# Two-layer LoRA product in one pass: the start of the first block product is put in another order

## The reference

```python
# layer 0: ids 0, W0 = L0 base_weight, A0, B0 picked per batch entry
x = x + (x @ W0.T + b0) + (x @ A0[ids].T) @ B0[ids].T
# layer 1: W1, A1, B1, SCALING = 2
x = x + (x @ W1.T + b1) + 2 * (x @ A1[ids]) @ B1[ids]
```

## Time and profile before

| | us |
|---|---|
| median of 3 runs | 2081.53 (2079.79 to 2082.87) |
| profiled execution, its own time | 2081.34 |
| its span, first to last instruction | 2079.6 |
| TensorE busy in the span | 2054.9 (99%) |
| first matmul of step 0 | 19.7 |

### The profile page before, as it was taken

The page is one execution under the profiler, slowest core; times in us unless marked ns, Lnnn a source line. Parts: engine busy times, 40 slices in busy tenths (PEclk is TensorE's granted clock), DMA queues, the critical chain, the costliest instruction groups (busy, mean ns, idle before and its releaser), DMA issues.

```text
span 2079.6 us, 27886 instructions
## 1 busy us (share of the span) xinstructions
PE 2054.9 (99%) x9372; PEld 1709.6 (82%) x9372; DVE 1588.2 (76%) x2180; ACT 725.5 (35%) x1291; POOL 717.3 (34%) x513
## 2 busy tenths in 40 slices
PE   6999999999999999999999999999999999999999
PEld 6887888888888888888888888888888888888887
DVE  5688868877888887677877677877687886777895
ACT  5572323323333333333333333333333333333332
POOL 2134414551304552213544131545040445131443
PEclk9999999999999999999999999999999999999999
DMA  9986748995737795746796655798564789474676
GB/s 295 283 313 176 249 139 260 285 297 158 239 109 242 241 315 175 216 126 207 235 311 215 186 170 163 225 296 273 146 214 135 215 267 321 145 220 119 218 218 195
DMA packets 283898, 458.03 MB, mean 220 GB/s; under 512 B 27500, under 2 KB 88940, under 8 KB 283244
## 3 DMA queue, kind: packets, MB, share of 16 engines
q1 hardware_dynamic: 215788, 333.54, 52.1%
q10 hardware_dynamic: 67968, 122.71, 19.3%
HBM read 382.75 MB, written 74.45 MB: 220 GB/s over the span
## 4 chain that ended last, share of the span: by engine, by line
PE 90%; DVE 3%; issue 1%; DMA 1%; SPq 0%; POOL 0%; ACT 0%; DVEq 0%; POOLq 0%; ACTq 0%
PE acc L1568 28%; PE acc L1574 28%; PE acc L1579 28%; PE h_acc L1492 2%; PE h_acc L1496 2%; PE acc L1506 1%; PE h_acc L1495 1%; DVE w_lo L1083 0%; DVE vp_lo L1078 0%; DMA w_raw<-v_t 0%; DVE c_acc L1191 0%; DMA x_pre<-w_t 0%; DVE xop_lo L1109 0%; DVE x_sum L1098 0%; DVE c_out L1261 0%
## 5 line engine op out<-in xcount | busy, mean ns | idle before, releaser
L893 POOL TENSOR_TENSOR w_raw<-w_raw,w_second 128x512 f32<-128x512 f32 x464 | 654.5, 1411 | 1222.8 <-DMA w_second<-wc_t 696.1
L1083 DVE TENSOR_TENSOR w_lo<-w_raw,w_hi 128x512 fp32r<-128x512 f32 x672 | 582.0, 868 | 420.3 <-ACT w_hi L930 417.7
L930 ACT ACTIVATE w_hi<-w_raw 128x512 fp32r<-128x512 f32 x672 | 424.3, 632 | 1234.7 <-PE acc L1579 1048.5
L1568 PE MATMUL acc<-xop_hi,w_hi 128*128 128x512 f32 x2688 | 726.1, 391 | 1.1 <-DVE c_pre L1261 1.1
L1574 PE MATMUL acc<-xop_lo,w_hi 128*128 128x512 f32 x2688 | 723.2, 390 | 0.0
L1579 PE MATMUL acc<-xop_hi,w_lo 128*128 128x512 f32 x2688 | 722.0, 390 | 0.0
L1579 PEld LDWEIGHTS acc<-xop_hi,w_lo 128*128 128x128 f32 x2688 | 503.9, 188 | 104.0
L1574 PEld LDWEIGHTS acc<-xop_lo,w_hi 128*128 128x128 f32 x2688 | 504.1, 188 | 103.3
L1568 PEld LDWEIGHTS acc<-xop_hi,w_hi 128*128 128x128 f32 x2688 | 503.3, 188 | 103.8 <-ACT w_hi L930 1.5
L1109 DVE TENSOR_TENSOR xop_lo<-x_sum,xop_hi 128x512 fp32r<-128x512 f32 x240 | 158.5, 681 | 3.8 <-ACT xop_hi L943 3.0
L1261 DVE TENSOR_TENSOR c_out<-acc,c_out 128x512 f32<-128x512 f32 x224 | 149.7, 680 | 4.4 <-PE acc L1506 3.8
(11 more groups left out here) (105 smaller groups left out, 1017.9 us busy)
## 6 DMA issues: line engine op xcount, KB each, us to landing
w_raw<-wc_t SPq DMA_DIRECT2D x448, 256.0 KB, 3.9
w_second<-wc_t ACTq DMA_DIRECT2D x320, 256.0 KB, 4.4
w_raw<-v_t SPq DMA_DIRECT2D x208, 256.0 KB, 4.2
w_second<-v_t ACTq DMA_DIRECT2D x144, 256.0 KB, 4.8
x_in<-x_t SPq DMA_DIRECT2D x128, 256.0 KB, 5.8
out_t<-c_out SPq DMA_DIRECT2D x128, 256.0 KB, 5.3
w_part<-w_t SPq DMA_DIRECT2D x32, 512.0 KB, 8.0
x_pre<-w_t SPq DMA_DIRECT2D x64, 256.0 KB, 6.0
```

What stands on the lines that cost most here:

```text
L893: nc.gpsimd.tensor_tensor(w_raw[:, r, :], w_raw[:, r, :], w_second[:, n % RAW2, :], ALU.add if sign > 0 else ALU.subtract).then_inc(w_summ ...
L930: nc.scalar.activation(flat(w_hi[:, s % RING, :, :]), w_raw[:, r, :], ACT.Copy).then_inc(w_hi_ready, 1)
L1083: nc.vector.tensor_tensor(flat(w_lo[:, s % RING, :, :]), w_raw[:, s % RAW, :], f(flat(w_hi[:, s % RING, :, :])), ALU.subtract).then_inc(w_ ...
L1568: nc.tensor.matmul(bank[:, :], w_hi[:, s % RING, kk, :], xop_hi[:, place, :], start=(k == 0), stop=False)
```

## The change

What moves (step numbers are TensorE's):

- Transposes of the identity, whose result nobody reads (`keep_clock`): 16 ahead of parts 0 and 1, 20 behind them.
- The turn of parts: none in step 1, two parts in each step from 2 to 15; pair 4 now ahead of pair 3 but behind pair 2. Groups of 4 transposes behind 6, 8, 10 and 12 matmuls (step 0: 4, 5, 8, 10).
- A1 products: those of parts 0 to 3 in steps 2 and 3 instead of 1 and 2; the later ones still two steps behind the turn. The first of a step stands behind 8 matmuls, the second behind all 12. The split of a part stands in the step of its product instead of one step before.
- b0_rows are turned in step 2 (`B_IN`): two banks in its middle, two behind it.
- X's first four tiles have DMAs and a semaphore of their own, issued right behind parts 0 and 1; parts 2 and 3 come next, then X's second half, two of the eight a1 DMAs, parts 4 and 5, the stores of parts 0 and 1, and only then b0_rows. The ids go from ScalarE's queue.
- ScalarE splits X's first tiles around w_split_hi(0), copies parts 2 and 3 before a1_hi, and splits X's tiles 4 to 7 after a1_hi and split_part_hi(0). b1_hi moves from the end of its iteration 3 to the end of iteration 4, behind e_hi; b0t's splits and the store of b0t move from 2 to 3.

```diff
+    A1_BY_ACT = 6
-    B_AFTER, E_AFTER, Q_AFTER = (0, 1), 3, (5, 6)
+    B_IN, E_AFTER, Q_AFTER = 2, 3, (5, 6)
-    TURN_AT = ((0, (-1, -1, 0, 0)), (1, (1, 1, 2, 2)), (4, (3, 3, 4, 4)), (2, (5, 5, 6, 6)), (5, (7, 7, 8, 8)),
-               (3, (9, 9, 10, 10)), (6, (11, 11, 12, 12)), (7, (13, 14, 15, 15)))
+    TURN_AT = ((0, (-1, -1, 0, 0)), (1, (2, 2, 3, 3)), (2, (4, 4, 5, 5)), (4, (6, 6, 7, 7)), (3, (8, 8, 9, 9)),
+               (5, (10, 10, 11, 11)), (6, (12, 12, 13, 13)), (7, (14, 14, 15, 15)))
-    PART_G_AT = [max(at + 2, 1) for _, _, at in PARTS]
+    PART_G_AT = [2, 2, 3, 3] + [at + 2 for _, _, at in PARTS[4:]]
-        return [n for n in range(2, NPART) if PART_G_AT[n] == g + 1]
+        return [n for n in range(2, NPART) if PART_G_AT[n] == g]
...
# SyncE, start
             for n in range(2):
                 load_part(n)
-            for k in range(KH):
-                load_x(0, 1, 1, k)
+            row = KH * P
+            for o in range(TT):
+                sp.dma_start(flat(x_pre[:, 3, o, 0:KS, :]), w1_t[TT + o, :, row:row + SW]).then_inc(x_first_loaded, 16)
             for n in range(2, PIN):
                 load_part(n)
+            for o in range(TT):
+                load_x(0, 1, 1, 2 * o + 1)
             sp.wait_ge(ids_loaded, 32)
+            for b in range(A1_BY_ACT, BATCH):
+                sp.dma_start(a1_raw[:, b, :, :], ...).then_inc(a1_sp_loaded, 16)
+            for n in PARTS_AT[-1]:
+                load_part(n + PIN)
+            for n in PARTS_AT[-1]:
+                store_part(n)
             for b in range(BATCH):
                 sp.dma_start(b0_rows[b * RANK:(b + 1) * RANK, :], ...).then_inc(b0_loaded, 16)
...
# ScalarE, start
+            for n in PARTS_AT[0]:
+                for mm in range(2):
+                    copy_part(n, mm)
+            act_e.wait_ge(a1_loaded, A1_BY_ACT * 16)
+            act_e.wait_ge(a1_sp_loaded, (BATCH - A1_BY_ACT) * 16)
             nc.scalar.activation(a1_hi[:, :, :, :], ...)
+            split_part_hi(0)
+            for k in range(KS, KH):
+                x_split_hi(0, k)
...
# TensorE
+            def keep_clock(n):
+                for _ in range(n):
+                    nc.tensor.transpose(h_acc[:, 0:P], ident[:, :], ident[:, :])
             pe.wait_ge(ident_made, 2)
+            keep_clock(16)
             for n in PARTS_AT[-1]:
                 for mm in range(2):
                     turn_part(n, mm)
+            keep_clock(20)
...
-                    for n in range(NPART):
-                        if PART_G_AT[n] == s:
-                            add_part_g(n)
-                    turn_at = {0: (), 2: (0, 6), 4: (0, 3, 6, 9) if s > 0 else (0, 1, 2, 3)}[len(turns)]
+                    turn_at = {0: (), 2: (0, 6), 4: (6, 8, 10, 12) if s > 0 else (4, 5, 8, 10)}[len(turns)]
+                    products = [n for n in range(NPART) if PART_G_AT[n] == s]
...
# behind the matmuls with xop_lo, ahead of those with w_lo
+                    for n in products[:1]:
+                        add_part_g(n)
+                    if s == B_IN:
+                        pe.wait_ge(b0_loaded, BATCH * 16)
+                        for n in range(2):
+                            turn(n, [...])
...
# behind the step
+                    for n in products[1:]:
+                        add_part_g(n)
+                    turn_before(3 * KS)
+                    if s == B_IN:
+                        for n in range(2, 4):
+                            turn(n, [...])
```

More of the change, by code:

```diff
@@ L756, in _ @@
                     load_w(s)
-                if g < 2:
-                    for b in range(4 * g, 4 * g + 4):
+                if 1 <= g < 3:
+                    for b in range(4 * (g - 1), 4 * g):
                         sp.dma_start(b1_rows[b * RANK:(b + 1) * RANK, :],
@@ L940, in x_split_hi @@
                 else:
-                    wait_x(act_e, q, 0)
+                    if q == 0 and k < KS:
+                        act_e.wait_ge(x_first_loaded, 16 * KS)
+                    else:
+                        wait_x(act_e, q, 0)
                     src = x_tile(q, 0, k)
@@ L1004, in load_second @@
                                 ).then_inc(wb_loaded[n % RAW2], 16)
+            for l, ids_d in enumerate((ids0, ids1)):
+                act_e.dma_start(ids[0:1, l, :], ids_d.rearrange("(o n) -> o n", o=1)).then_inc(ids_loaded, 16)
             act_e.wait_ge(ident_made, 2)
@@ L1009, in _ @@
             act_e.wait_ge(ids_loaded, 32)
-            for b in range(BATCH):
+            for b in range(A1_BY_ACT):
                 slot = act_e.value_load(ids[0:1, 1, b:b + 1], min_val=0, max_val=SLOTS - 1)
@@ L1031, in _ @@
                 pl, i = divmod(q, NPROD)
+                for n in PARTS_AT[g] if g == B_IN else []:
+                    for mm in range(2):
+                        copy_part(n, mm)
                 if g + 2 < NG:
@@ L1034, in _ @@
                 load_second(g + 2 + RAW2)
+                if g == 1:
+                    split_part_hi(1)
+                for n in PART_ENDS:
+                    if PART_G_AT[n] == g - 1:
+                        copy_part_g(n)
                 for n in parts_split(g)[:1]:
                     split_part_hi(n)
-                for n in PART_ENDS:
-                    if PART_G_AT[n] == g:
-                        copy_part_g(n)
                 for n in parts_split(g)[1:]:
                     split_part_hi(n)
[L1042 to L1045, removed]
+                if g == 3:
                     act_e.wait_ge(t_copied, 4)
@@ L1050, in _ @@
                                          .broadcast_to([P, KT, 2]), ACT.Copy).then_inc(b0t_hi_ready, 1)
+                for n in PARTS_AT.get(g, []) if g not in (0, B_IN) else []:
+                    for mm in range(2):
+                        copy_part(n, mm)
                 if g == 3:
@@ L1053, in _ @@
                     a_split_hi(0)
+                if g == 4:
+                    act_e.wait_ge(e_masked, 1)
+                    nc.scalar.activation(e_hi[:, :], e_bd[:, :], ACT.Copy).then_inc(e_hi_ready, 1)
                     act_e.wait_ge(b1_loaded, BATCH * 16)
@@ L1186, in scale_c @@
                 if k == 0:
-                    dve.wait_ge(x_loaded[block_no(half, th)], (pl + 1) * 16 * KH)
+                    wait_block(dve, block_no(half, th), pl)
                     if half == pl:
@@ L1274, in _ @@
                     nc.vector.tensor_copy(v_part[:, n, mm, :], part_bank[mm][:, :]).then_inc(part_copied, 1)
[L1275 to L1278, removed]
+            w_split_lo(0)
             for k in range(KS):
                 x_split_lo(0, k)
+            w_split_lo(1)
             dve.wait_ge(a1_hi_ready, 1)
@@ L1289, in _ @@
                 pl, i = divmod(q, NPROD)
+                if g in (B_IN, B_IN + 1):
+                    for n in range(2 * (g - B_IN), 2 * (g - B_IN) + 2):
+                        t_copy(n, flat(b0t_raw[:, 4 * n:4 * n + 4, :]))
                 if g + 2 < NG:
@@ L1296, in _ @@
                         evict(qq, m)
+                if g == 1:
+                    split_part_lo(1)
                 for n in parts_split(g):
                     split_part_lo(n)
[L1299 to L1302, removed]
+                if g == 3:
                     dve.wait_ge(t_copied, 4)
@@ L1575, in _ @@
                                          start=False, stop=False)
+                    for n in products[:1]:
[3 more added lines that the diff above has]
+                        for n in range(2):
+                            turn(n, [b0_rows[:, (4 * n + i) * P:(4 * n + i + 1) * P] for i in range(4)])
                     pe.wait_ge(w_lo_ready, s + 1)
```

51 lines of the change are left out of this document (22 added, 29 removed).

## The result

The changed kernel takes 2114.41 us, median of 5 runs (2112.33 to 2115.53), against 2081.77 (2079.79 to 2082.87) for the kernel before, also 5 runs: ratio 1.0153, 95% interval 1.0142 to 1.0164. It is 32.6 us slower, far outside the predicted range, which ended at 2090. The profiled span is 2112.7 us against 2079.6. A change of 0.2%, 4.2 us, is about what a single run can tell.

A forecast was written before the change was run, and what follows sets the result against it. TensorE, busy 99% of the span, was taken as the bound, so only idle time and clock could change. 2081.34 + 2.45 (make_q later) + 1.6 + 0.8 (clock) - 1.3 (steps 6 to 17) gave 2084.9 us, range 2076.5 to 2090.

The forecast's parts named there:

- Steps 6 to 17: Later steps: short waits of 2.5 us in all replace 3.8 us lost before, 1.3 us gained.
- The text's own sign of being wrong: Wrong if make_q starts at 66 or below, or if steps 6 to 17 idle for much over 3 us.
- Clock: Slow clock behind TensorE's idle stretches: 1.6 us a fall; 1.6 for step 5, 0.8 for step 2; bounds 0 and 6.4.
- Start: Step 0 starts at 13.25, not 19.7, and ends near 18.35 with a warm clock; head start 9.7 us.
- Before step 2: TensorE idles from 21.1 to 24.7 for ScalarE's list up to w_hi(2); product 0 ends at 28.7.
- B0's rows: Middle of step 2: b0 lands at 31.1 (bounds 28.0 and 33.4), so TensorE idles from 28.7.
- the rival in which the transposes do not count: Start: idle transposes do not warm the clock, step 0 runs at half clock, product 0 ends at 31.6; 2085.4 us; chance 0.10.
- Step 5: Product 6 waits for vp_lo(6) from 61.5 to 65.0, 3.5 us idle; make_q starts at 70.25.
- Idle transposes: Start: 36 at 0.22 us, 7.9 us, end at 12.9, before step 0 at 13.25; costed at nothing.
- The head start is spent: At make_q: 75.0 with 4.75 us of moved work counted, against 72.57 before, 2.45 us later.
- slow clock: Rival: each idle stretch over 1.4 us up to step 5 drops the clock, no later gain; 2090.2 us; chance 0.22.
- head start survives: Rival: b0 lands by 28.7, no clock falls in steps 2 and 5, later wait gone; -4.3, 2077.1 us; chance 0.18.

The follow-up runs named there:

- experiment 1: Kernel before, with only the late places of products, turns and splits from step 6 on: 2105.21 us, 21.6 above the kernel before.
- experiment 2: Changed kernel with products, turns and splits from step 6 on back in their old places: 2083.44 us, 0.2 from the kernel before.
- experiment 5: Changed kernel with b1_hi moved behind the splits of iteration 5: 2112.54 us, 1.9 less.
- experiment 3: Changed kernel with ScalarE's splits of X and a ahead of the second part's copies in steps 10 to 15: 2101.74 us, 12.7 less.
- experiment 4: Changed kernel with GpSimd's residual additions of the first product cut to one column in 128: 2113.61 us, no change.
- experiment 6: Changed kernel without the 36 idle transposes: 2112.65 us, 1.8 less.
- experiment 8: Changed kernel with turns from step 6 on behind 0, 3, 6 and 9 matmuls again, products and splits left late: 2102.13 us, 12.3 less.
- experiment 9: Changed kernel with splits for products of step 6 on one step ahead again, products and turns left late: 2104.74 us, 9.7 less.
- experiment 10: Kernel of experiment 2 plus b1_hi late, 46 idle transposes and part 2's split between copies of parts 4 and 5: 2079.52 us, ratio 0.9993.
- experiment 7: Changed kernel with 46 instead of 20 idle transposes behind part 1: 2114.95 us.

## Why the prediction was wrong

**The step that failed is "Steps 6 to 17"**, forecast at 1.3 us of gain with bounds of 3.8 gained and 2 lost, measured at 27.85 lost. It let "copy_part_g (0.4), vp_hi and vp_lo need 2.9 us behind the last product", with an eviction where there is one. That is not the list. What counts is everything that ScalarE and VectorE have between the step's last copy and the end of the split: at step 15 7.3 us, from 166.76 to 174.02. The rows for it were in the trace of before, where the same list takes the same 7.26 us; the wait of 2.22 us at 159.63, which the forecast counted as saved, was this chain. The change took the slack away in two ways at once: the last turn, and with it the last copy, went to the end of the step, and the split went from the step before into the product's own. The product's later place gave back only two thirds of a step. The bounds came from the same short list, so the range could not hold the result either, and none of the rivals was this chain. The text's own sign of being wrong (idle of much over 3 us in steps 6 to 17) is what came: 23.74 us. In experiment 1 these places alone cost 21.6 us, and in experiment 2 their removal gives back 31. The middle stretches give 22.9 and 30.4 us for the same two; of the difference, 3.5 us are idle time and 4.0 busy time at a lower clock. Part of it goes with the turns: the old lists turn one part in each of steps 13 and 14, the new ones two, and the waits in steps 14 and 15 are 0 and 0.74 us in experiment 1 against 1.38 and 5.01. The rest was not settled.

**Clock.** A fall was priced at 1.6 us, and two were counted. The middle stretch has 7.0 us of it, all set off by waits that the forecast did not have. In step 5 the fall did come, at 1.4 us by experiment 5. The rows are steps 5, 11, 12 (no fall) and 16: TensorE alone (length, busy, granted clock, DMA share, GB/s), changed kernel:

```profile
66.80:69.60 2.80, 2.76 (x13) 0.50 0.07 6
...
128.30:131.30 3.00, 3.00 (x14) 0.50 0.76 290
139.88:143.00 3.12, 3.12 (x24) 1.00 0.06 19
189.00:191.80 2.80, 2.72 (x12) 0.50 0.99 359
```

**The early part was nearly right**, 5.57 us lost against 4.85. The changed kernel and experiments 3, 4, 6, 8 and 9, whose code is the same up to step 5 but for the idle transposes in 6, have make_q between 72.35 and 73.75, so this does not hang on one run. *Start*: step 0 at 13.02 (13.25 said), but at 1.2 GHz, so it ended at 20.37 and not 18.35. *Before step 2*: idle to 26.10, put down to w_hi, 1.4 us later than said. *B0's rows*: said to land at 31.1, and TensorE to wait for them from 28.7. The last of their loads was issued at 26.2 and took 5.1 us, so the landing was forecast well. TensorE was not: it came to them only at 31.28, because step 2 began 1.4 us late and at the low clock, and it did not wait. Where it came earlier, it did wait, until 30.49 in experiment 8 (1.14 us) and until 30.75 in experiment 4 (0.28 us). The time is also that of the rival in which the transposes do not count (31.6), yet that was not its reason: they do count, and the pause behind them undid it.

*Step 2 on*: wait to 41.59 (40.7 said). *Step 4*: 1.54 us idle for the eviction (1.5 said), starting at 53.78 (51.7). *Step 5*: 3.12 us idle (3.5 said), and vp_lo as its cause, ending at 66.84 (65.0). make_q at 73.39 was just above the 70 to 73 named. *Idle transposes* at nothing held within what a single run tells (experiment 6), though not as worked out: at 0.22 us each they were to fill the time up to 12.9, but with the clock risen the last 20 took 0.12 each and ended at 9.88. "The head start is spent" held as well: with the late places back, experiment 2 is level with before, and even in experiment 10 make_q is no earlier once the moved 4.75 us are counted.

The rivals *slow clock* and *head start survives* were about this early part and differ by a few us; against 27.85 they did not matter.

## What to carry to other kernels

When work is moved within a step, write out each producing engine's whole list from the last event it must wait for to the result that is needed, not only the operations of the value itself; here 1.2 us of vp_lo stood behind 4.9 us of unrelated work. A split made one step ahead of its use is the slack that makes such a list harmless: giving it up, together with a later last event, cost 1.5% here, and undoing one of the two alone gave back about a third and moved the rest to other waits. When two kernels are compared at a mark such as make_q, count the work that has moved past the mark first: in experiment 10, 4.7 us of head start were 4.75 us of moved work. And where a gain in an early stage is not seen at the end, look at idle and busy time apart: in experiments 5 and 7 the idle time of the later stage stayed at 23.7 to 23.8 us, and what ate the gain was busy time at the lower clock.

## What the runs showed of the hardware

- Transposes do raise the clock. 16 of them from 1.44 us on, with nothing else on TensorE, brought four turns from 0.88 to 0.58 us, and 46 behind part 1 kept step 0 at 5.17 us in place of 7.35, its first four matmuls at 1.17 us in place of 2.07 (in experiment 10, with the same 46, these took 1.54). The Trainium skill (TensorE: Matmul & The Clock Gate, Part 4: PE-mode transpose) says that the full clock does not engage for transpose mode, as it does not count as busy in the same way; these fp32 transposes disagree with it, and the measurement decides. The trace lists them as MATMUL and does not show their mode.
- The granted clock is no sign at the very start. In experiment 6 it reads 1.00 over all of step 0, whose first four matmuls take 2.08 us; durations tell the clock there.
- Which pause makes the clock fall varies. It had fallen behind pauses of 2.04 us (ahead of 127.47), 3.12 and 5.45 us, but not by 143 us behind one of 3.19 us. Behind the pause of 1.54 us ahead of step 4 it held in the changed kernel (four matmuls in 1.17 us) and fell in experiment 10. The timeline and the window of TensorE alone, experiment 10:

```profile
49.76 2.03 PE L1618 MATMUL acc<-xop_hi,w_hi 128*128 128x512 f32 x4 [1.54 <-DVE c_out L1278]
...
49.80:52.50 2.70, 2.70 (x7) 0.50 0.99 374
```

- VectorE's pair of vp_lo takes 3.43 us beside a sum of GpSimd and 2.35 without it (experiment 4).
